# A unit's exponentials on ScalarE, taken ahead of the split of the next unit's loaded q and k

## The chip, the cores and the metric

One Trainium2 chip, one core of it. The metric is the device time of one execution in microseconds (us), lower is better; three runs of the kernel before are there, and one more execution under the profiler. TensorE, VectorE, ScalarE, GpSimd and SyncE stand as PE, DVE, ACT, POOL and SP.

## The reference, cut to what matters

Four layers, each a residual cross-attention followed by a residual feed-forward part, over x of 8 x 128 tokens x 512. Layers 0, 1 and 3 attend with 32 query heads on 8 key heads of width 128 (layer 0 with rotary positions, 1 and 3 with RMS-normed q and k):

```python
q = rope_or_rmsnorm(x @ Wq); k = rope_or_rmsnorm(ctx @ Wk); v = ctx @ Wv   # 32 / 8 / 8 heads of 128
probs = softmax(q @ k.T / sqrt(128) + mask)        # per batch and head, 128 x 128
x = x + tanh(gate) * (probs @ v) @ Wo
x = x + tanh(gate) * ffn(layernorm(x))
```

## The kernel before

An attention layer of this kind is done in 64 **units** u: one key head g (four query heads, so q is 128 x 512 and k is 128 x 128) for one batch b. Matmuls take each operand as a high and a low part (`_h`, `_l`: ScalarE copies the high part, and VectorE or GpSimd subtracts it from the source). What feeds a unit's score matmuls are `qT_h`, `qT_l` and both halves of `kT`.

The order on every engine is written out by hand, in numbers. Iteration i of the outer list holds steps of several units; `self.at(i, order, name, layer, u)` places a step, the steps of an iteration are sorted by `order`, and each of the five engine programs walks the same sorted list and issues what it has under that name. An engine therefore runs its own parts strictly in this order, and a wait at the head holds all that is behind it. A unit begins in its iteration i and ends some six iterations later.

For the 52 units u = 8 to 59 of layers 0, 1 and 3 (`TURNED_BY_DMA`) q, k and the probabilities are turned (transposed) by way of DRAM:

- i + 1: VectorE transposes 32 x 32 blocks of q and k into `xn` (`blocks_q`), SP stores them to `between_q` (`store_q`), and later loads them as `q_in` (`load_q`, order 72).
- i + 2: `split_k` at 13 and `split_q` at 13.5: ScalarE waits for the load, in layers 1 and 3 scales the keys in place (`q_in<-q_in`), copies `kT` and `qT_h`; VectorE makes the low part of `kT`, GpSimd `qT_l`. `scores` at 70.5 is on TensorE.
- i + 3: `mask` at 4 on VectorE (it writes S and the negated row maximum `nmx`); `exp` on ScalarE, four instructions, W and `den` from S and `nmx`; then `rden` on VectorE (it stands behind `times_v` there), the product `W<-W,rden` on GpSimd (`probs`, 40), its block transposition `S<-W` on VectorE (`blocks_p`, 42) and the store to `between_p` on SP (`store_p`, 42); `load_p` at 73.
- i + 4: `split_p` at 45 (`pT_h` on ScalarE, `pT_l` on GpSimd); i + 5: `times_v` at 20 (`oT_h` on ScalarE, `oT_l` on VectorE); i + 6: `attn_out` at 0 on TensorE.

So in one iteration ScalarE meets `exp` of unit u, the split of q and k of unit u + 1, and `oT_h` of unit u - 2; in the same iteration SP issues the store of unit u's probabilities, and behind it the load of q and k of unit u + 2. Weights come as halves of pieces into `raw` and are split to `ring_h` (ScalarE) and `ring_l` (GpSimd) by `next` steps, at 15 and 90 of an iteration in the steady part of a layer:

```python
for order in ((71, 90) if i < 7 else (15, 90) if i in self.steady else (5, 24, 46, 90)):
    self.at(i, order, "next", i + order / 100, "dve" if order == 46 else "pool")
```

During layer 0, every second iteration from 16 on also has `clear_slots` at 47: SP issues a DMA that clears 1030 KB of DRAM, ahead of `load_q`.

Of the kernel before, what the change touches and what calls it, by code (L numbers as in the profile page):

```python
# [91 lines left out]
class Schedule:  # L92
# [44 lines left out]
    def attention(self, layer, first, base):  # L137
        lag = 6
        units = [(g, b) for g in range(G) for b in range(NB)]
        self.first[layer], self.units[layer] = first, units  # L140
        for u, (g, b) in enumerate(units):
            i = first + u
            if b == 0:
                row = base + 5 * g
                keys_values, *queries = self.need((row + 2, row, row + 1), i, 70)
                five = [*queries, keys_values, *self.need(range(row + 3, row + 5), i + lag, 0)]
            self.five[layer, u] = five
            last = b == NB - 1
            ahead = (layer, u) in AHEAD
            early = layer == 3 and u < 2  # L150
            self.at(*((first - 1, 5) if early else (i, 45 if ahead else 70)), "keys_values", layer, u,
                    needs=[five[2], self.ctx[b]])
            self.at(i, 45 if ahead else 70, "project", layer, u, needs=five[0:2],
                    frees=[(n, "qkv", (layer, u), i + 0.7) for n in five[0:3]] if last else ())
            if KINDS[layer] == "norm":
                self.at(i + 1, 6 if layer == 1 and u < NB else 10, "normalise", layer, u)
            if (layer, u) in TURNED_BY_DMA:
                self.at(i + 1, 10.2 if KINDS[layer] == "norm" else 11, "blocks_q", layer, u)
                self.at(i + 1, 12, "store_q", layer, u)
                self.at(i + 1, 72, "load_q", layer, u)  # L160
                self.at(i + 2, 13, "split_k", layer, u)
                self.at(i + 2, 13.5, "split_q", layer, u)
                self.at(i + 2, 70.5, "scores", layer, u)
                self.at(i + 3, 4, "mask", layer, u)
                self.at(i + 3, 16, "exp", layer, u)
                self.at(i + 3, 40, "probs", layer, u)
                self.at(i + 3, 42, "blocks_p", layer, u)
                self.at(i + 3, 42, "store_p", layer, u)
                self.at(i + 3, 73, "load_p", layer, u)
                self.at(i + 4, 45, "split_p", layer, u)  # L170
            else:
                self.at(i + 1, 72 if (layer, u - 1) in TURNED_BY_DMA else 50, "turn_q", layer, u)
                self.at(i + 1, 72 if (layer, u - 1) in TURNED_BY_DMA else 50, "split_k", layer, u)
                self.at(i + 2, 40, "scores", layer, u)
                self.at(i + 2, 56, "mask", layer, u)
                self.at(i + 2, 71, "exp", layer, u)
                self.at(i + 3, 9, "probs", layer, u)
                if (layer, u) in TURNED_BY_PE:
                    self.at(i + lag - 2, 46 if u == 0 and (layer, 1) in AHEAD else 30, "turn_p", layer, u)
                else:  # L180
                    self.at(i + 3, 21, "blocks_p", layer, u)
                    self.at(i + 3, 21, "store_p", layer, u)
                    self.at(i + 3, 62, "load_p", layer, u)
                    self.at(i + lag - 2, 60, "split_p", layer, u)
            self.at(i + lag - 1, 20, "times_v", layer, u)
            self.at(i + lag, 0, "attn_out", layer, u, needs=five[3:5],
                    frees=[(n, "attn_out", (layer, u), i + lag) for n in five[3:5]] if last else ())
            self.at(i + lag, 10.5 if KINDS[layer] == "norm" or i + lag - 1 - first in range(NB, LAST_BY_DMA + 1) else 0,
                    "add_out", layer, u)
            if NB <= u < len(units) - NB:  # L190
                self.steady.add(i)
        return [first + units.index((G - 1, b)) + lag for b in range(NB)]
# [2467 lines left out]
```

## Time and profile before

| what | value |
|---|---|
| median of 3 runs | 2883.64 us (2881.02 to 2886.97) |
| the profiled execution | 2890.32 us, its span 2888.5 us |
| busy in the span: PE, DVE, POOL, ACT | 2438.5, 1860.4, 1553.4, 1213.2 us |
| TensorE's granted clock, mean | 0.935 |
| DMA | 390.33 MB, 135 GB/s |

The span is the time from the first to the last instruction in the trace. An engine's busy time says nothing of which wait sets the pace; idle times before an instruction and what released it do, and these are read per unit in the next parts.

### The profile page before, as it was taken

How to read it: one execution, taken by the hardware profiler on the slowest of the kernel's cores; microseconds unless marked ns; L12 is line 12 of the kernel's file. 1: busy time of each engine (PE TensorE's matmuls, PEld its weight loads, DVE VectorE, ACT ScalarE, POOL GpSimd, SP SyncE). 2: the span in 40 equal slices, each digit the busy share in tenths (PEclk: the TensorE clock that was granted, in tenths of full speed). 3: DMA queues.
4: the chain of work that ended last, by engine and by line, in shares of the span. 5: the costliest groups of instructions: out<-in, count | busy, mean ns of one | idle time of the engine just before them, and what ended most of it. 6: DMA issues, size and time to landing. Idle time of an engine off the chain costs nothing. (4 is left out here: it accounts for less than half of the span.)

```text
span 2888.5 us, 40547 instructions
## 1 busy us (share of the span) xinstructions
PE 2438.5 (84%) x12225; PEld 1996.1 (69%) x12225; DVE 1860.4 (64%) x3505; ACT 1213.2 (42%) x3610; POOL 1553.4 (54%) x1624
## 2 busy tenths in 40 slices
PE   5888888888888888889788888799788888889877
PEld 4777777676677777777666677676567777777753
DVE  4766666666887666666676676563376666666762
ACT  2433333333424455555542445323235555555420
POOL 4565565565424566666542666541446666666433
PEclk8998888889999999999999999899889999999989
DMA  3345555555313444444431000148624444444254
GB/s 103 94 157 176 169 194 172 177 172 172 126 63 116 156 147 146 148 150 149 139 128 45 16 1 1 42 161 310 241 63 138 149 152 152 148 142 144 93 194 164
DMA packets 296365, 390.33 MB, mean 135 GB/s; under 512 B 20977, under 2 KB 195697, under 8 KB 293210
## 3 DMA queue, kind: packets, MB, share of 16 engines
q1 hardware_dynamic: 280416, 338.60, 36.1%
q0 software_dynamic: 10224, 42.03, 4.2%
q10 hardware_dynamic: 5514, 7.11, 0.8%
q8 instruction: 105, 1.72, 0.2%
q14 instruction: 106, 0.87, 0.1%
HBM read 269.92 MB, written 151.49 MB: 146 GB/s over the span
## 5 line engine op out<-in xcount | busy, mean ns | idle before, releaser
L2252 POOL TENSOR_TENSOR qT_l<-q_in,qT_h 128x512 fp32r<-128x512 f32 x156 | 203.6, 1305 | 380.1 <-ACT qT_h L1197 379.3
L898 PE MATMUL B_s<-kT,qT_h 128*128 128x256 f32 x768 | 215.9, 358 | 174.5 <-POOL qT_l L2252 151.4
L1376 ACT ACTIVATE W<-S,nmx 128x128 f32<-128x128 f32 x768 | 297.6, 393 | 63.6 <-DVE nmx L1703 63.3
L1522 DVE TENSOR_TENSOR oT_l<-B_three,oT_h 128x512 fp32r<-128x512 f32 x200 | 137.2, 686 | 285.5 <-ACT oT_h L1197 285.3
L898 PEld LDWEIGHTS B_s<-kT,qT_h 128*128 128x128 f32 x768 | 154.8, 202 | 229.1 <-POOL qT_l L2252 198.7
L2292 POOL TENSOR_TENSOR W<-W,rden 128x512 f32<-128x512 f32 x192 | 200.1, 1042 | 204.9 <-DVE rden L1708 204.8
L841 PE MATMUL B_out<-ring_h,oT_h 128*128 128x512 f32 x516 | 230.6, 447 | 40.7 <-DVE oT_l L1522 34.8
L1197 ACT ACTIVATE q_in<-q_in,wqk 128x128 f32<-128x128 f32 x104 | 55.2, 531 | 488.2 <-DMA q_in<-between_q 488.2
L1718 DVE STREAM_TRANSPOSE S<-W 128x512 f32<-128x512 f32 x184 | 130.6, 710 | 188.0 <-POOL W L2292 187.8
L2298 POOL TENSOR_TENSOR pT_l<-W,pT_h 128x512 fp32r<-128x512 f32 x184 | 238.6, 1297 | 21.3 <-ACT pT_h L1197 21.2
L2228 POOL TENSOR_TENSOR ring_l<-raw,ring_h 128x512 fp32r<-128x512 f32 x166 | 214.3, 1293 | 62.7 <-ACT ring_h L1197 62.6
L841 PE MATMUL B_out<-ring_l,oT_h 128*128 128x512 f32 x516 | 217.6, 422 | 0.0
L841 PE MATMUL B_out<-ring_h,oT_l 128*128 128x512 f32 x516 | 216.7, 420 | 0.0
L1197 ACT ACTIVATE kT<-q_in 128x128 fp32r<-128x128 f32 x156 | 67.5, 433 | 353.0 <-DMA q_in<-between_q 349.7
L899 PE MATMUL B_s<-kT,qT_l 128*128 128x128 f32 x768 | 178.2, 232 | 0.0
L899 PEld LDWEIGHTS B_s<-kT,qT_l 128*128 128x128 f32 x768 | 158.4, 206 | 2.1
L841 PEld LDWEIGHTS B_out<-ring_h,oT_h 128*128 128x128 f32 x516 | 106.3, 206 | 74.0 <-DVE oT_l L1522 46.8
L2239 POOL TENSOR_TENSOR rn<-rn,pw 128x5 f32<-128x5 f32 x128 | 149.8, 1170 | 10.7
L1728 DVE SCALAR_TENSOR_TENSOR X<-B_out,gates,X 128x512 f32<-128x512 f32 x200 | 145.2, 726 | 11.4 <-PE B_out L841 11.4
L841 PE MATMUL B_qkv<-ring_h,xnT_h 128*128 128x512 f32 x348 | 142.8, 410 | 11.4 <-DVE spare_l L1522 4.8
L1376 ACT ACTIVATION_READ_ACCUMULATOR W<-S,nmx 128x1 f32 x768 | 144.8, 188 | 0.0
L1522 DVE TENSOR_TENSOR kT<-q_in,kT 128x128 fp32r<-128x128 f32 x156 | 84.2, 539 | 91.9 <-ACT kT L1197 91.9
(504 smaller groups left out, 7901.3 us busy)
## 6 DMA issues: line engine op xcount, KB each, us to landing
raw<-in_pieces SPq DMA_DIRECT2D x270, 256.0 KB
between_q<-xn SPq DMA_DIRECT2D x156, 320.0 KB, 2.9
q_in<-between_q SPq DMA_DIRECT2D x156, 320.0 KB, 3.2
between_p<-S SPq DMA_DIRECT2D x184, 256.0 KB, 2.1
W<-between_p SPq DMA_DIRECT2D x184, 256.0 KB, 3.0
slots_x<-in_zero SPq DMA_DIRECT2D x32, 1030.0 KB, 5.9
raw<-in_experts SPq DMA_DIRECT2D x16, 768.0 KB, 7.3
w<-in_experts SPq DMA_DIRECT2D x8, 1024.0 KB, 15.9
```

Of the source, the lines that this page charges most:

```text
L841: t = pe.matmul(dst, a, b, start=first and n == 0, stop=last and n == len(steps) - 1)
L898: pe.matmul(B_s[:, cols(r, 2 * P)], qT[0][:, cols(r)], kT_both[:, :], start=True, stop=False)
L899: t = pe.matmul(B_s[:, cols(2 * r)], qT[1][:, cols(r)], kT[0], start=False, stop=True)
L1376: t = act.activation(probs_r, scores_r, ACT.Exp, bias=nmx[:, k, r:r + 1], accum_out=den[:, k, r:r + 1])
L1522: return dve.tensor_tensor(dst, a, b, ALU.subtract)
L1718: dve.transpose(blocks_first(S[:, k, :]), W[:, k, :].rearrange("p (r j q) -> p r j q", r=R, q=BLOCK)).then_inc(*blocks_made.now((layer, u)))
L1728: dve.scalar_tensor_tensor(out=X[:, b, 0:D], in0=bank[:, :], scalar=factor, in1=X[:, b, 0:D], op0=ALU.mult, op1=ALU.add).then_inc(*x_add.n ...
L2228: pool.tensor_tensor(lo, landing_place(item), f32(hi), ALU.subtract).then_inc(*piece_lo["pool"].now(i))
L2239: pool.tensor_tensor(rn[:, k, 0:R + 1], rn[:, k, 0:R + 1], pw[:, 0:R + 1], ALU.pow).then_inc(*rms.now((layer, u)))
L2252: pool.tensor_tensor(heads_first(qT[1][:, :]), queries_in, heads_first(f32(qT[0][:, :])), ALU.subtract).then_inc(*q_low.now((layer, u)))
L2292: pool.tensor_tensor(W3, W3, rden[:, k, :].unsqueeze(2).to_broadcast([P, R, P]), ALU.mult).then_inc(*probs.now((layer, u)))
L2298: pool.tensor_tensor(heads_first(pT[1][:, :]), by_block(W[:, k, :]), heads_first(f32(pT[0][:, :])), ALU.subtract).then_inc(*p_split.now((l ...
```

## The change

One number of the list: `exp` of a unit that is turned by DMA goes from order 16 to 12.5 of the same iteration.

```diff
                 self.at(i + 2, 13.5, "split_q", layer, u)
                 self.at(i + 2, 70.5, "scores", layer, u)
                 self.at(i + 3, 4, "mask", layer, u)
-                self.at(i + 3, 16, "exp", layer, u)
+                self.at(i + 3, 12.5, "exp", layer, u)
                 self.at(i + 3, 40, "probs", layer, u)
```

No instruction is added or taken away. Only ScalarE has a part under `exp`; VectorE's `rden` goes by the step of its own. On ScalarE the four exponentials now stand ahead of the next unit's k and q (orders 13, 13.5) and of the weight split at 15. This holds for 153 units, 51 of each of the layers 0, 1 and 3; the orders of the other four engines are the same as before.

ScalarE in layer 0 before, two iterations, the first with a weight split at 15 and the second without (`B_three` is a PSUM bank, `ring_lent_h` the high part of weights):

```order
L1197 ACTIVATE kT<-q_in 128x128
L1197 ACTIVATE qT_h<-q_in 128x512
L1197 ACTIVATE ring_lent_h<-raw 128x512
L1376 ACTIVATE W,den<-S,nmx 128x128 x4
L1197 ACTIVATE oT_h<-B_three 128x512
L1197 ACTIVATE pT_h<-W 128x512
L1197 ACTIVATE v_h<-B_three 128x128
L1197 ACTIVATE kT<-q_in 128x128
L1197 ACTIVATE qT_h<-q_in 128x512
L1376 ACTIVATE W,den<-S,nmx 128x128 x4
```

The same engine and place in the changed kernel:

```order
L1376 ACTIVATE W,den<-S,nmx 128x128 x4
L1197 ACTIVATE kT<-q_in 128x128
L1197 ACTIVATE qT_h<-q_in 128x512
L1197 ACTIVATE ring_lent_h<-raw 128x512
L1197 ACTIVATE oT_h<-B_three 128x512
L1197 ACTIVATE pT_h<-W 128x512
L1197 ACTIVATE v_h<-B_three 128x128
L1376 ACTIVATE W,den<-S,nmx 128x128 x4
L1197 ACTIVATE kT<-q_in 128x128
L1197 ACTIVATE qT_h<-q_in 128x512
```

The four exponentials have passed the two copies of the next unit and the weight split; `oT_h` is behind all of them both times.

GpSimd in layer 1 (`rn` are the scales of the RMS norm), the same before and after; two iterations with a weight split between `qT_l` and W, then one without:

```order
L2252 TENSOR_TENSOR qT_l<-q_in,qT_h 128x512
L2228 TENSOR_TENSOR ring_lent_l<-raw,ring_lent_h 128x512
L2292 TENSOR_TENSOR W<-W,rden 128x512
L2298 TENSOR_TENSOR pT_l<-W,pT_h 128x512
L2236 TENSOR_SCALAR rn<-ss 128x5
L2239 TENSOR_TENSOR rn<-rn,pw 128x5
L2228 TENSOR_TENSOR ring_lent_l<-raw,ring_lent_h 128x512
L2252 TENSOR_TENSOR qT_l<-q_in,qT_h 128x512
L2292 TENSOR_TENSOR W<-W,rden 128x512
```

Nothing moves here: the product of unit u stands behind `qT_l` of unit u + 1, whose input ScalarE now makes later.

## Rows read from the trace of the kernel before

**Rows 1.** The page: the chain that ended last, by line

```profile
DMA q_in<-between_q 6%; POOL qT_l L2252 2%; POOL W L2292 2%; DMA out_x<-rows_last 2%; DMA slots_y<-S 1%; DVE S L1718 1%; PE B_qkv L841 1%; ACT qT_h L1197 1%; POOL ring_l L2228 1%; ACT q_in L1197 1%; DVE X L1728 1%; SPq L2437 1%; PE B_out L841 1%; POOL ring_lent_l L2228 1%; PE B_three L1093 1%
```

**Rows 2.** Waits in layer 1, 960 to 1300 us: total us, times, longest

```profile
POOL W L2292 <- DVE rden L1708: 35.2, 33, 1.6
PE B_s L898 <- POOL qT_l L2252: 28.5, 31, 5.3
```

**Rows 3.** Timeline, layer 1, iteration with weight split: start, us, instruction, [idle <-releaser]

```profile
1236.33 0.69 DVE L1703 TENSOR_REDUCE nmx<-S 128x4 f32<-128x512 f32 x1
...
1243.70 0.71 DVE L1718 STREAM_TRANSPOSE S<-W 128x512 f32<-128x512 f32 x1 [1.15 <-POOL W L2292]
...
1246.67 0.69 DVE L1703 TENSOR_REDUCE nmx<-S 128x4 f32<-128x512 f32 x1
...
1237.68 0.53 ACT L1197 ACTIVATE q_in<-q_in,wqk 128x128 f32<-128x128 f32 x1 [4.50 <-DMA q_in<-between_q]
...
1239.62 0.39 ACT L1376 ACTIVATE W<-S,nmx 128x128 f32<-128x128 f32 x1
...
1241.16 0.58 ACT L1197 ACTIVATE oT_h<-B_three 128x512 fp32r<-128x512 f32 x1
...
1248.16 0.53 ACT L1197 ACTIVATE q_in<-q_in,wqk 128x128 f32<-128x128 f32 x1 [4.63 <-DMA q_in<-between_q]
...
1242.62 1.04 POOL L2292 TENSOR_TENSOR W<-W,rden 128x512 f32<-128x512 f32 x1 [0.74 <-DVE rden L1708]
```

**Rows 4.** Timeline, layer 1, the iteration ahead of it, without weight split

```profile
1226.45 0.69 DVE L1703 TENSOR_REDUCE nmx<-S 128x4 f32<-128x512 f32 x1
...
1227.85 0.53 ACT L1197 ACTIVATE q_in<-q_in,wqk 128x128 f32<-128x128 f32 x1 [5.07 <-DMA q_in<-between_q]
...
1230.81 0.58 ACT L1197 ACTIVATE oT_h<-B_three 128x512 fp32r<-128x512 f32 x1
...
1232.28 1.04 POOL L2292 TENSOR_TENSOR W<-W,rden 128x512 f32<-128x512 f32 x1 [1.53 <-DVE rden L1708]
```

**Rows 5.** Timeline of PE in the same two iterations

```profile
1230.81 0.39 PE L898 MATMUL B_s<-kT,qT_h 128*128 128x256 f32 x1 [0.62 <-POOL qT_l L2252]
...
1232.17 0.50 PE L841 MATMUL B_out<-ring_h,oT_h 128*128 128x512 f32 x1 [0.23 <-DVE oT_l L1522]
...
1240.70 0.39 PE L898 MATMUL B_s<-kT,qT_h 128*128 128x256 f32 x1 [0.63 <-POOL qT_l L2252]
...
1242.52 0.50 PE L841 MATMUL B_out<-ring_h,oT_h 128*128 128x512 f32 x1 [0.68 <-DVE oT_l L1522]
```

**Rows 6.** Timeline, layer 0, no clear ahead of the load: without and with weight split

```profile
608.46 0.69 DVE L1703 TENSOR_REDUCE nmx<-S 128x4 f32<-128x512 f32 x1
...
608.90 0.43 ACT L1197 ACTIVATE kT<-q_in 128x128 fp32r<-128x128 f32 x1 [5.11 <-DMA q_in<-between_q]
...
612.77 1.04 POOL L2292 TENSOR_TENSOR W<-W,rden 128x512 f32<-128x512 f32 x1 [1.53 <-DVE rden L1708]
...
658.16 1.04 POOL L2292 TENSOR_TENSOR W<-W,rden 128x512 f32<-128x512 f32 x1 [0.75 <-DVE rden L1708]
```

**Rows 7.** Timeline, layer 0, a clear ahead of the load: with and without weight split

```profile
603.49 1.04 POOL L2292 TENSOR_TENSOR W<-W,rden 128x512 f32<-128x512 f32 x1 [0.84 <-DVE rden L1708]
...
617.75 0.69 DVE L1703 TENSOR_REDUCE nmx<-S 128x4 f32<-128x512 f32 x1
...
621.75 0.43 ACT L1197 ACTIVATE kT<-q_in 128x128 fp32r<-128x128 f32 x1 [7.51 <-DMA q_in<-between_q]
...
624.14 0.57 ACT L1197 ACTIVATE oT_h<-B_three 128x512 fp32r<-128x512 f32 x1
...
625.60 1.04 POOL L2292 TENSOR_TENSOR W<-W,rden 128x512 f32<-128x512 f32 x1 [1.56 <-DVE rden L1708]
```

**Rows 8.** PE's timeline, then windows (us, busy of PE, PEld, DVE, ACT, POOL, PEclk, DMA)

```profile
1335.97 0.65 PE L841 MATMUL B_out<-ring_h,oT_h 128*128 128x512 f32 x1 [0.78 <-DVE oT_l L1522]
...
1336.20:1339.50 3.30, 3.30 (x9) 2.52 (x9) 2.31 (x5) 0.26 (x2) 2.92 (x4) 0.50 0.48 160
```

## The prediction

> **What bounds the kernel now.** I began with the chain that ended last: its largest line is the load of q and k from DRAM, 6% of the span [rows 1], so the units turned by DMA are the place to look. The waits of a stretch of layer 1 show that GpSimd waits for `rden` in every one of 33 iterations, 35.2 us in all, and that TensorE waits for `qT_l` in 31 of them, 28.5 us [rows 2]. Then I followed one iteration in the timeline. q lands at 1237.68; the scaling, `kT`, `qT_h` and a weight split run until the first exponential at 1239.62; `oT_h` starts at 1241.16, 1.54 us later; `rden` and the product W follow at 1242.62, the block transposition at 1243.70 to 1244.41, and 3.75 us after its end the next q is there, at 1248.16 [rows 3]. That is a closed cycle of 10.48 us: load, split, exponentials, product, transposition, store, load. The four exponentials lie in it with 1.54 us.
>
> They need not. They wait for `nmx`, and VectorE ends it at 1247.36, 2.95 us after the same transposition [rows 3]. Call d the time from the end of `nmx` to the arrival of q. It is 0.80 us here and 0.66 in the iteration ahead of it (1237.68 less 1237.02) [rows 3]. Both ends hang on the transposition, so d will not change much when the cycle does.
>
> **The change step by step.** No work is added; one block of 1.54 us changes places with the split, on ScalarE alone. Two things follow in an iteration.
>
> *The `rden` side.* Before, exponentials end at q + K + 1.54, where K is the time of the split (1.42 us in rows 4 after taking 1.54 from 1230.81 less 1227.85; 1.94 with a weight split, 1239.62 less 1237.68 in rows 3). After, `oT_h` starts at the later of (nmx + 0.04 + 1.54) and q, plus K; the 0.04 is my allowance for the semaphore. So `oT_h`, `oT_l`, `rden` come d earlier, at most 1.54; with d below 0 they come later.
>
> *The `qT_l` side.* `qT_h` waits for the exponentials, so it and `qT_l` on GpSimd come later by δ = 1.58 - d, or 0 if q is later than that. W stands behind `qT_l`, and behind `ring_l` where the iteration has a weight split, and GpSimd was idle for a time g ahead of W. W can therefore come forward by the smaller of (gain of `rden`) and (g - δ). The rest of the cycle starts with W, so this is the gain of the iteration.
>
> Layers 1 and 3, no weight split: q at 1227.85, `nmx` ends 1227.14, d = 0.71, δ = 0.87, g = 1.53 [rows 4]: the smaller of 0.71 and 0.66. Over the 34 such iterations with d between 0.38 and 1.06 this averages 0.72: **24.6 us**.
> With weight split: d = 0.66, δ = 0.92, g = 0.74 [rows 3]: W comes 0.18 us *later*. Where d is 0.80 it is about level. Over 55 iterations the average is -0.10: **-5.2 us**. Here the weight split on GpSimd eats what ScalarE gives.
> Seven iterations of these layers have q over 2 us late (the first ones of a layer among them): 4 without split give 1.55, 3 with it 0.84: **8.7 us**. Six near the ends have `nmx` later than q, and lose 0.2 to 1.5: **-4.6 us**.
>
> Layer 0 has two kinds in turn. With a clear ahead of the load, q lands at 621.75 while `nmx` ended at 618.44 [rows 7]: the exponentials are over long before, δ is 0, and `oT_h` goes from 624.14 to 622.60. Without weight split GpSimd's idle 1.56 us lets W follow by 1.54 to 1.56, with one the idle 0.84 us is all that there is [rows 7]. 7 x 1.55 + 17 x 0.79 = **24.3 us**.
> Without a clear, VectorE has rotary products to do ahead of the mask and q is *earlier* than `nmx`: 608.90 against 609.15, d = -0.25 [rows 6]. Then δ = 1.83, and W moves by 1.53 - 1.83 = -0.30; with a weight split (idle 0.75) by -1.1 [rows 6]. 15 iterations average -0.38 and 12 average -1.07: **-18.5 us**.
>
> Sum: 24.6 - 5.2 + 8.7 - 4.6 + 24.3 - 18.5 = 29.3 us less. The counts and averages are over all 153 iterations, with each one's own d and g; the rows are typical ones.
>
> *What could eat it on TensorE.* Its work in an iteration is 1240.70 less 1230.81 less the idle 0.63 and 0.23, so 9.03 us [rows 5]. The iteration without split goes from 9.83 (1237.68 less 1227.85) to some 9.17: it still fits, barely. Scores start δ later, but they had idle time behind them at `attn_out`, 0.68 us with the split and 0.23 without [rows 5], and the mask that needs them is far: `nmx` starts at 1246.67 behind two mask steps of 0.7 us each, so the mask at about 1245.2, while the scores started at 1240.70 [rows 3, 5] and take 1.2. So I price it at nothing, and if that cover fails it is the second rival.
> What remains is the clock. The idle times of 0.63 and 0.68 around the scores become one of about 1.4 us ahead of them. Before, TensorE was at 1.2 GHz (granted 0.50) for 1336.20 to 1339.50, behind an idle time of 0.78 us and one like it just before [rows 8]; so idle time of this sum does drop it now and then, and then half of 3.3 us of work is lost, 1.65, of which the iteration with split has 10.4 - 9.0 = 1.4 spare. At one in ten of the 55, 0.3 us each, that is 2 us. I take 1.5.
>
> From the profiled execution's 2890.32 us (span 2888.5 and 1.8 around it) this gives 2862.5; the median of the runs is 6.7 us below it, so I forecast 2883.64 - 28 = **2856 us**.
>
> **Rivals.**
> *GpSimd's order doesn't hold it (W follows `rden` alone).* Then every iteration of layers 1 and 3 gains d, with split too: 89 x 0.72 = 64, and the late ones 31 x 1.54 = 48, less 27 x 0.30 + 5 = 13: some 100 us, 2784. For it: W is released by `rden` in all 33 iterations [rows 2]. Against: it comes after `qT_l` in the list, and with idle of 0.74 against a delay of 0.92 `rden` is no longer the last. The Trainium skill says in "Perfetto Trace Analysis", Tensor Engine Instruction, that ScalarE, VectorE and GpSimd are strict FIFO, which would exclude this; no row of before shows W ready and held. 0.03.
>
> *TensorE sets the pace (slower).* The place is the start of the scores. If each δ there is passed on, less the idle at `attn_out`, the iterations with split lose 0.88 - 0.68 = 0.20, 55 x 0.20 = 11 us, and those without 0.83 - 0.23 = 0.60, 34 x 0.60 = 20: 31 us slower, 2915. It decides where the projection's end, not `qT_l`, releases the next scores; now `qT_l` does, after 0.62 us idle [rows 5], and TensorE has 1.4 us to spare in an iteration with split. What speaks for it is 31 waits of 33 for `qT_l` [rows 2]: they are where TensorE loses time, and the change makes them longer. The Trainium skill's advice in the same page, Optimization Strategies, is of this kind: speed up what keeps the matmul engine waiting. By that advice this change is the wrong way round. The cycle in rows 3 says otherwise, since `scores` isn't in it. 0.12.
>
> *Gains and losses cancel.* If d shrinks by 0.3 us everywhere (loads landing earlier against VectorE, or `nmx` late by scores), 89 iterations of layers 1 and 3 lose 0.3 each from both sides, 27 us, and nothing is left: 2883. The averages with split and in layer 0 show how near zero many are. 0.10.
>
> *Clock.* If half of the 55 iterations with split fall to 1.2 GHz, and each loses 0.3, and the neighbours without split, which have nothing spare, take the full 1.65 in one of four: 8 + 14 us, 2878. 0.10.
>
> **How the numbers follow.** My forecast has 0.65 and its own range is 2846 to 2868 (d off by 0.1 moves it by 9; layer 0's losses by half, 9). The range of 2840 to 2890 takes in cancelling and the clock and leaves out most of the slower rival and the 100 us one. A difference under 0.2%, 6 us, can't be told from none. Faster: 0.65 + 0.03 + 0.09 of the clock case and a little of cancelling, 0.78. Same 0.09, slower 0.13.
>
> **What would show it.** In the changed trace: ScalarE's exponentials released by `nmx` and ended before q or at most 1 us behind it; W released by `qT_l` or `ring_l` with no idle time in iterations with split, and nearly so without; periods of 9.2 us without split in layer 1 and an unchanged 10.4 with; in layer 0 the iteration behind a clear shorter by 0.8 to 1.5, the other longer by 0.3 to 1.1; TensorE idle 1.3 us ahead of the scores and nearly none ahead of `attn_out`. I would be wrong if d turns out to shrink, if the scores come to be released by the projection in most iterations, or if the 0.50 clock spreads in layers 1 and 3.

## The result and the profile after

The changed kernel takes 2849.43 us (median of 4 runs, 2841.56 to 2853.46); the kernel before, on the same chip, 2882.33 us. The ratio is 0.9883, with an interval of 0.9855 to 0.991: 1.2% less, 33 us. The profiled execution took 2853.46 us, 36.9 less than that of before.

The page of the changed kernel: span, busy times, the chain that ended last (by engine, by line), and two of its groups of instructions.

```profile
span 2851.6 us, 40547 instructions
...
PE 2408.4 (84%) x12225; PEld 1979.2 (69%) x12225; DVE 1849.1 (65%) x3505; ACT 1220.0 (43%) x3610; POOL 1543.3 (54%) x1624
...
ACT W L1376 5%; POOL qT_l L2252 4%; PE B_qkv L841 4%; POOL W L2292 4%; DMA slots_y<-S 3%; DVE S L1700 2%; DVE ss L1614 2%; DVE nmx L1703 2%; ACT qT_h L1197 2%; DVE S L1697 2%; DMA q_in<-between_q 2%; DMA out_x<-rows_last 2%; ACT q_in L1197 2%; PE B_out L841 1%; POOL ring_l L2228 1%
...
L1376 ACT ACTIVATE W<-S,nmx 128x128 f32<-128x128 f32 x768 | 300.3, 397 | 775.9 <-DVE nmx L1703 775.8
...
L2292 POOL TENSOR_TENSOR W<-W,rden 128x512 f32<-128x512 f32 x192 | 199.9, 1041 | 39.2 <-DVE rden L1708 38.5
```

The load of q led the chain with 6% [rows 1]; it has 2% now, and the exponentials (`W L1376`), `qT_l` and the product W stand at the top. The exponentials' idle time is released by `nmx`, nearly all of it. The product's idle time is 39.2 us over its 192 units, where the page of before has 204.9.

The waits of layer 1, 960 to 1300 us, changed kernel (total us, times, longest):

```profile
ACT W L1376 <- DVE nmx L1703: 145.7, 34, 5.0
POOL qT_l L2252 <- ACT qT_h L1197: 107.6, 34, 4.0
DVE S L1718 <- POOL W L2292: 52.5, 34, 1.8
...
PE B_s L898 <- POOL qT_l L2252: 32.3, 29, 2.4
```

The wait of the product for `rden`, 35.2 us in 33 iterations [rows 2], is gone: it has no row any more. TensorE's wait for `qT_l` is longer in sum, 32.3 us where [rows 2] have 28.5.

Two iterations of layer 1 in the timeline of the changed kernel, with a weight split, then without one:

```profile
1179.74 0.40 ACT L1376 ACTIVATE W<-S,nmx 128x128 f32<-128x128 f32 x1 [4.52 <-DVE nmx L1703]
...
1181.30 0.53 ACT L1197 ACTIVATE q_in<-q_in,wqk 128x128 f32<-128x128 f32 x1
...
1182.89 1.26 POOL L2252 TENSOR_TENSOR qT_l<-q_in,qT_h 128x512 fp32r<-128x512 f32 x1 [2.62 <-ACT qT_h L1197]
1183.24 0.57 ACT L1197 ACTIVATE oT_h<-B_three 128x512 fp32r<-128x512 f32 x1
...
1184.12 1.28 POOL L2228 TENSOR_TENSOR ring_l<-raw,ring_h 128x512 fp32r<-128x512 f32 x1
1184.21 0.39 PE L898 MATMUL B_s<-kT,qT_h 128*128 128x256 f32 x1 [1.58 <-POOL qT_l L2252]
...
1185.37 1.03 POOL L2292 TENSOR_TENSOR W<-W,rden 128x512 f32<-128x512 f32 x1
...
1186.43 0.71 DVE L1718 STREAM_TRANSPOSE S<-W 128x512 f32<-128x512 f32 x1 [1.81 <-POOL W L2292]
...
1189.40 0.69 DVE L1703 TENSOR_REDUCE nmx<-S 128x4 f32<-128x512 f32 x1
...
1190.12 0.40 ACT L1376 ACTIVATE W<-S,nmx 128x128 f32<-128x128 f32 x1 [4.51 <-DVE nmx L1703]
...
1191.68 0.52 ACT L1197 ACTIVATE q_in<-q_in,wqk 128x128 f32<-128x128 f32 x1
...
1193.26 1.30 POOL L2252 TENSOR_TENSOR qT_l<-q_in,qT_h 128x512 fp32r<-128x512 f32 x1 [2.61 <-ACT qT_h L1197]
1194.55 1.04 POOL L2292 TENSOR_TENSOR W<-W,rden 128x512 f32<-128x512 f32 x1
```

ScalarE's first instruction on q (`q_in<-q_in`, which scales the keys) starts right behind the last exponential, with no idle time: the 4.50 us of waiting for the load [rows 3] have moved ahead of the exponentials, where they are a wait for `nmx`. On GpSimd `qT_l`, `ring_l` and W now run back to back (1182.89 to 1186.40), so the product has no slack left. The iteration without a split has lost its 1.53 us of idle time [rows 4] too. TensorE waits 1.58 us ahead of the scores where [rows 5] have 0.63.

The rows from one product to the next, 1185.37 to 1194.55, also show what sets the pace now. W and its transposition are over at 1187.14; VectorE ends the mask steps and `nmx` at 1190.09; the exponentials run to 1191.68; scaling, `kT` and `qT_h` until `qT_l` starts at 1193.26; W follows at 1194.55. That is a second closed cycle, of 9.18 us, with no load in it, and with a weight split `ring_l` is in it too, 1.25 us (1184.12 to 1185.37), which makes 10.4. The exponentials have left the cycle of the load, but they are in this one. In layers 1 and 3, 28 of the 34 iterations without a split lie within 0.05 us of 9.20, and 48 of the 55 with one within 0.05 us of 10.38; ScalarE still waited for the load in 7 of these 89, where before it did in all of them. The chain that ended last, from 2300 to 2400 us (layer 3), before and then after:

```profile
by line: DMA q_in<-between_q 31.6%; issue 16.7%; POOL qT_l L2252 13.3%; POOL W L2292 10.5%; DVE S L1718 7.2%; ACT qT_h L1197 6.3%; ACT q_in L1197 5.4%; POOL ring_l L2228 5.1%; SPq L2437 3.2%; POOL ring_lent_l L2228 1.2%; SPq L2457 0.3%; ACT
...
by line: issue 17.0%; POOL qT_l L2252 12.7%; ACT W L1376 12.4%; POOL W L2292 10.5%; DVE ss L1614 7.0%; DVE S L1700 6.3%; DVE nmx L1703 6.3%; ACT qT_h L1197 6.2%; DVE S L1697 5.5%; DMA q_in<-between_q 4.8%; ACT q_in L1197 4.0%; POOL ring_l L
```

Layer 0 in the changed kernel: an iteration without a clear ahead of its load, then one behind a clear.

```profile
601.74 0.40 ACT L1376 ACTIVATE W<-S,nmx 128x128 f32<-128x128 f32 x1 [6.03 <-DVE nmx L1703]
...
603.30 0.41 ACT L1197 ACTIVATE kT<-q_in 128x128 fp32r<-128x128 f32 x1
...
604.31 1.29 POOL L2252 TENSOR_TENSOR qT_l<-q_in,qT_h 128x512 fp32r<-128x512 f32 x1 [1.93 <-ACT qT_h L1197]
605.60 1.04 POOL L2292 TENSOR_TENSOR W<-W,rden 128x512 f32<-128x512 f32 x1
...
611.30 0.40 ACT L1376 ACTIVATE W<-S,nmx 128x128 f32<-128x128 f32 x1 [5.69 <-DVE nmx L1703]
...
614.54 0.43 ACT L1197 ACTIVATE kT<-q_in 128x128 fp32r<-128x128 f32 x1 [1.59 <-DMA q_in<-between_q]
...
616.86 1.04 POOL L2292 TENSOR_TENSOR W<-W,rden 128x512 f32<-128x512 f32 x1
```

Behind the clear the exponentials are over 1.59 us before q lands, where q came after 7.51 us of idle time and the exponentials followed it [rows 7]. In the other kind ScalarE is held by `nmx` until 601.74, and the copies stand behind the exponentials.

I measured each iteration as the time from the product W ahead of it to its own. Averages by kind, us, before and after:

| kind of iteration | count | before | after | sum | forecast |
|---|---|---|---|---|---|
| layers 1 and 3, no weight split | 34 | 9.92 | 9.32 | -20.3 | -24.6 |
| layers 1 and 3, weight split | 55 | 10.42 | 10.46 | +2.3 | +5.2 |
| layers 1 and 3, q over 2 us behind `nmx` | 7 | | | -11.4 | -8.7 |
| layers 1 and 3, near the ends | 6 | | | +2.3 | +4.6 |
| layer 0 behind a clear, no split | 7 | 13.50 | 11.88 | -11.4 | -24.3 with the next row |
| layer 0 behind a clear, split | 17 | 14.16 | 13.14 | -17.3 | |
| layer 0 without a clear, no split | 15 | 9.42 | 9.77 | +5.3 | +18.5 with the next row |
| layer 0 without a clear, split | 12 | 9.79 | 10.76 | +11.7 | |

The sum is 38.8 us less; over the same iterations, from product to product, the stretch of layer 0 went from 593.9 to 582.2 us, that of layer 1 from 550.6 to 535.8, that of layer 3 from 530.5 to 518.0, together 39.0. The other stages gave back 2.

### The profile page after: what moved, and what is told of

Read it like the earlier page. It is cut to its first block, busy times and chain, and to the rows that moved or that the text cites. A ratio compares the mean times of both kernels' runs of the same rounds, so it can differ in the third digit from the quotient of the medians.

```text
span 2851.6 us, 40547 instructions
## 1 busy us (share of the span) xinstructions
PE 2408.4 (84%) x12225; PEld 1979.2 (69%) x12225; DVE 1849.1 (65%) x3505; ACT 1220.0 (43%) x3610; POOL 1543.3 (54%) x1624
## 4 chain that ended last, share of the span: by engine, by line
DVE 15%; POOL 14%; PE 11%; issue 10%; ACT 10%; DMA 8%; ACTq 0%; SPq 0%; DVEq 0%; POOLq 0%
ACT W L1376 5%; POOL qT_l L2252 4%; PE B_qkv L841 4%; POOL W L2292 4%; DMA slots_y<-S 3%; DVE S L1700 2%; DVE ss L1614 2%; DVE nmx L1703 2%; ACT qT_h L1197 2%; DVE S L1697 2%; DMA q_in<-between_q 2%; DMA out_x<-rows_last 2%; ACT q_in L1197 2%; PE B_out L841 1%; POOL ring_l L2228 1%
## 5 line engine op out<-in xcount | busy, mean ns | idle before, releaser
L1376 ACT ACTIVATE W<-S,nmx 128x128 f32<-128x128 f32 x768 | 300.3, 397 | 775.9 <-DVE nmx L1703 775.8
L898 PE MATMUL B_s<-kT,qT_h 128*128 128x256 f32 x768 | 217.2, 360 | 220.2 <-POOL qT_l L2252 196.6
L2298 POOL TENSOR_TENSOR pT_l<-W,pT_h 128x512 fp32r<-128x512 f32 x184 | 238.5, 1296 | 20.3 <-ACT pT_h L1197 20.2
L2292 POOL TENSOR_TENSOR W<-W,rden 128x512 f32<-128x512 f32 x192 | 199.9, 1041 | 39.2 <-DVE rden L1708 38.5
L1522 DVE TENSOR_TENSOR kT<-q_in,kT 128x128 fp32r<-128x128 f32 x156 | 61.3, 393 | 143.1 <-ACT kT L1197 143.1
L841 PE MATMUL B_qkv<-ring_h,xnT_h 128*128 128x512 f32 x348 | 142.5, 409 | 11.4 <-DVE spare_l L1522 4.8
L1376 ACT ACTIVATION_READ_ACCUMULATOR W<-S,nmx 128x1 f32 x768 | 144.5, 188 | 0.0
L1197 ACT ACTIVATE ring_h<-raw 128x512 fp32r<-128x512 f32 x190 | 117.5, 624 | 61.9 <-DMA raw<-in_pieces 37.8
L841 PE MATMUL B_qkv<-ring_l,xnT_h 128*128 128x512 f32 x348 | 140.4, 404 | 0.0
L841 PE MATMUL B_qkv<-ring_h,xnT_l 128*128 128x512 f32 x348 | 138.9, 399 | 0.0
```

The costliest lines, as they stand in the source:

```text
L841: t = pe.matmul(dst, a, b, start=first and n == 0, stop=last and n == len(steps) - 1)
L898: pe.matmul(B_s[:, cols(r, 2 * P)], qT[0][:, cols(r)], kT_both[:, :], start=True, stop=False)
L1197: return act.activation(dst, src, ACT.Copy, scale=scale)
L1376: t = act.activation(probs_r, scores_r, ACT.Exp, bias=nmx[:, k, r:r + 1], accum_out=den[:, k, r:r + 1])
L1522: return dve.tensor_tensor(dst, a, b, ALU.subtract)
L2292: pool.tensor_tensor(W3, W3, rden[:, k, :].unsqueeze(2).to_broadcast([P, R, P]), ALU.mult).then_inc(*probs.now((layer, u)))
```

## The experiments

The change edits line 165. "Before" is the kernel before, run on the same chip as each.

**One layer kind at a time.** `e1_norm_only` makes the change in layers 1 and 3 alone:

```diff
-                self.at(i + 3, 12.5, "exp", layer, u)
+                self.at(i + 3, 16 if layer == 0 else 12.5, "exp", layer, u)
```

> The exponentials go ahead of the split in layers 1 and 3 alone; layer 0 as before. Theory (each iteration gains the smaller of d and g less delta): the trace after gives 27 us of gain in layers 1 and 3 (my sum before had 23.5), so about 2855 us against 2882 before. Rival (layer 0's late loads give most of it): 2870 or more.

Measured: 2858.12 us, ratio 0.9908 (0.9875 to 0.9942), 29 us less. Layers 1 and 3 were as in the full change (9.32 and 9.24 us without a split, 10.38 and 10.40 with one), layer 0 as before. `e2_rope_only` makes it in layer 0 alone:

```diff
-                self.at(i + 3, 12.5, "exp", layer, u)
+                self.at(i + 3, 12.5 if layer == 0 else 16, "exp", layer, u)
```

> The exponentials go ahead in layer 0 alone. Theory: iterations behind a clear gain 0.8 to 1.6 us (24 of them, 24 to 29 us), the others lose 0.3 to 1.1 (17 us): net 6 to 12 us, about 2873. Rival (layer 0's losses are hidden by TensorE, so only gains count): 2857.

Measured: 2881.32 us, ratio 0.9981 (0.9961 to 1.0002), some 6 us less, an interval that just includes no change. By kind layer 0 gained and lost as in the full change (-11.6 and -14.8 behind a clear, +5.3 and +11.7 without). So layer 0 nearly cancels, and layers 1 and 3 give most of the result; 29 and 6 add up to 35, beside the 33 of the whole.

**Only where it helps.** `e6_behind_clear` keeps the new order in layers 1 and 3 and behind a clear, and the old one in the rest of layer 0:

```diff
-                self.at(i + 3, 12.5, "exp", layer, u)
+                self.at(i + 3, 16 if layer == 0 and i % 2 else 12.5, "exp", layer, u)
```

> The changed kernel, but in layer 0 the exponentials stay at 16 in the iterations whose load of q has no clear ahead of it (units with odd i). Theory: there q comes before nmx is done, so the new order only delays qT_h and loses 0.35 and 1.0 us in 15 and 12 iterations, 17 us; leaving it out gives 2849 - 17, about 2832 us. Rival (the loss and the gain of neighbours hang together): 2849.

Measured: 2834.96 us, ratio 0.9811 (0.9785 to 0.9837). The iterations without a clear were back at 9.37 and 9.85 us, those behind one stayed at 11.69 and 13.23. The loss of 17.0 us in the table above comes from the order there: taking it back gave 14 us by the medians, 21 by the ratios.

**Is it the weight split that eats the gain?** The split of a weight stands at order 15, between `qT_l` and the product on GpSimd. I moved it behind the product, in the kernel before (`e3_split_behind_w`) and in the changed one (`e4_both`):

```diff
-            for order in ((71, 90) if i < 7 else (15, 90) if i in self.steady else (5, 24, 46, 90)):
+            for order in ((71, 90) if i < 7 else (41, 90) if i in self.steady else (5, 24, 46, 90)):
```

> The kernel before, with the weight split of the steady iterations at order 41 instead of 15, so that ring_h stands behind oT_h on ScalarE and ring_l behind the product W on GpSimd. Theory of the closed cycle: ScalarE's 0.52 us of ring_h leaves the cycle in the 87 iterations with a split, and GpSimd's 1.3 us was in none (it was idle 0.74 us ahead of W): 45 us faster, about 2837. Rival (TensorE sets the pace): no change, 2882.

> The changed kernel with the weight split at order 41 as well. Theory (in the changed kernel an iteration with split is held by qT_l and ring_l on GpSimd, no longer by rden): iterations with split come to the period of those without, 10.46 to 9.32 us in 55 of layers 1 and 3, and about 1 us each in 29 of layer 0: some 90 us below the changed kernel's 2849, 2760. Rival (GpSimd's order is no limit, W follows rden alone): only ring_h's 0.52 us, 2805. Rival (TensorE sets the pace already): 2849.

Measured: `e3_split_behind_w` 2998.31 us, ratio 1.0388 (1.0356 to 1.042), slower where I expected faster; `e4_both` 2819.07 us, 0.9777 (0.974 to 0.9814), half of the gain over before that I expected. The trace of `e3_split_behind_w` shows what I had not counted: a step's DMA moves with it. Its timeline (SPq is the queue on which SyncE issues):

```profile
1240.23 1.28 POOL L2228 TENSOR_TENSOR ring_l<-raw,ring_h 128x512 fp32r<-128x512 f32 x1
...
1241.54 0.33 SPq L2430 DMA_DIRECT2D raw<-in_pieces  x1
...
1241.97 0.38 SPq L2437 DMA_DIRECT2D between_p<-S  x1
...
1242.46 0.37 SPq L2463 DMA_DIRECT2D q_in<-between_q  x1
...
1246.44 0.53 ACT L1197 ACTIVATE q_in<-q_in,wqk 128x128 f32<-128x128 f32 x1 [5.79 <-DMA q_in<-between_q]
```

The weight split issues the load of the next raw weight piece, which may overwrite `raw` only when `ring_l` is done at 1241.51. At order 41 it stands ahead of the store at 42, and the store of S, ready at 1241.02, is issued at 1241.97. q is used 5.4 us after the transposition's end instead of 3.75 [rows 3]. The edit had put a wait into the cycle of the load.

So `e8_before_43` and `e7_after_43` repeat it with 43 in place of 41, behind the store:

> The kernel before, weight split of the steady iterations at 43: behind the product W on GpSimd and behind the store of the probabilities on SP. My theory of order 41 failed by 160 us; what I now hold is that the raw load, which waits for ring_l, stood ahead of the store on SP and put store and next load 1.7 us back. With 43 the store is free and only the load of q waits some 0.4 us behind the raw load, about what ring_h gives back on ScalarE: 2875 to 2885. Rival (it is GpSimd's later pT_l, or ring_h ahead of pT_h, that costs): still over 2950.

> The changed kernel with the weight split at 43. Theory (GpSimd's order holds W back by ring_l in iterations with split, and order 41 gave back half of that on SP): their period falls to that without split, 10.45 to 9.3 us in 55 of layers 1 and 3, somewhat less in 29 of layer 0: 2770 to 2785. Rival (SP's raw load isn't what held order 41): 2819 as there.

Measured: `e8_before_43` 2915.13 us, 1.0086 (1.0055 to 1.0117); `e7_after_43` 2771.14 us, 0.9596 (0.9571 to 0.9621). `e7_after_43` is as expected; `e8_before_43` is 30 us above the 2885 that I gave as its upper end. With the split of the weight out of its way, the iteration with one went to 9.48 and 9.54 us in layers 1 and 3 of `e7_after_43`, beside 10.46 in the changed kernel. ScalarE's part of the weight split moved too, but that is 0.52 us, less than the 0.95 gained; and in the changed kernel `rden` was done 0.76 us ahead of W on average in these 55 iterations, while `ring_l` ran. That shows the step "the weight split on GpSimd eats what ScalarE gives". The same move of the exponentials is worth 1.2% with the weight split at 15 and 4.9% (0.9596 against 1.0086; 144 us by the medians) with it at 43.

Why `e8_before_43` still lost some 25 us, in its timeline:

```profile
1254.71 0.33 SPq L2437 DMA_DIRECT2D between_p<-S  x1
...
1255.22 0.33 SPq L2430 DMA_DIRECT2D raw<-in_pieces  x1
...
1255.66 0.41 SPq L2463 DMA_DIRECT2D q_in<-between_q  x1
...
1259.35 0.53 ACT L1197 ACTIVATE q_in<-q_in,wqk 128x128 f32<-128x128 f32 x1 [5.03 <-DMA q_in<-between_q]
```

The raw load now stands between the store and the load of q: 0.95 us from one issue to the other where it was 0.43, and 3.69 us from the issue to the use where it was 3.29. Over layers 1 and 3 it is alike: from the issue of the load of q to its landing the median is 3.71 us in the 56 loads with a raw load just ahead, and 3.22 in 101 loads of the kernel before. That is some 1.0 us more in the cycle of the load, against the 0.52 us that ScalarE's part of the split gives back: an estimate of 0.5 us each in 55 iterations, some 27 us in all, beside the 27.5 that this trace lost in the 89 ordinary iterations of these layers. In `e7_after_43` most of the same delay is hidden behind the exponentials; ScalarE waited for q in 32 of the 89, under 0.2 us on average over all.

**The rest of the chain ahead too.** If the exponentials needn't follow q, the sums, `rden`, the product, the transposition and the store needn't either. `e9_rden_w_ahead` moves the step that makes `rden` and W ahead of the split, the first of the three lines; `e5_w_ahead` the transposition and the store as well:

```diff
-                self.at(i + 3, 40, "probs", layer, u)
-                self.at(i + 3, 42, "blocks_p", layer, u)
-                self.at(i + 3, 42, "store_p", layer, u)
+                self.at(i + 3, 12.6, "probs", layer, u)
+                self.at(i + 3, 14, "blocks_p", layer, u)
+                self.at(i + 3, 14, "store_p", layer, u)
```

> The changed kernel with rden and the product W ahead of the next unit's split too (probs at 12.6, block transposition and store of the probabilities at 14). Theory (the exponentials are ready early, and only the order behind them keeps W back): W starts 0.3 us after the last exponential, the cycle through the load falls under TensorE's 9.03 us of work, and TensorE sets the pace at 9.1 to 9.3 us in all of layers 1 and 3: 75 us there, and 40 to 70 in layer 0, 2700 to 2735. Rival (TensorE or contention is near its limit already): above 2800.

> The changed kernel with rden and W at 12.6 only; block transposition and store stay at 42. Theory: W's place behind qT_l and ring_l was the hold; the transposition then waits for oT_l instead, 2.1 to 2.6 us after the last exponential where W is done at 1.35, and the store stands behind the raw load on SP. TensorE is the bound in layers 1 and 3 as before that costs anything: 2670 to 2710. Rival (order 14 of the transposition and the store is what gave the gain): above 2780.

Measured: `e5_w_ahead` 2666.88 us, 0.9237 (0.9207 to 0.9267), more than expected; `e9_rden_w_ahead` 2717.59 us, 0.9421 (0.9386 to 0.9456), a little above what was expected. From the timeline of `e5_w_ahead`:

```profile
1106.11 0.39 PE L898 MATMUL B_s<-kT,qT_h 128*128 128x256 f32 x1
...
1110.12 0.40 ACT L1376 ACTIVATE W<-S,nmx 128x128 f32<-128x128 f32 x1 [2.96 <-DVE nmx L1703]
...
1112.49 1.04 POOL L2292 TENSOR_TENSOR W<-W,rden 128x512 f32<-128x512 f32 x1 [3.12 <-DVE rden L1708]
...
1112.69 1.00 DVE L1522 TENSOR_TENSOR kT<-q_in,kT 128x128 fp32r<-128x128 f32 x1 [0.28 <-ACT kT L1197]
...
1113.49 1.35 POOL L2252 TENSOR_TENSOR qT_l<-q_in,qT_h 128x512 fp32r<-128x512 f32 x1
...
1114.89 0.39 PE L898 MATMUL B_s<-kT,qT_h 128*128 128x256 f32 x1
```

The product starts 2.37 us after the start of the first exponential; in the changed kernel it started 5.63 after it (1185.37 less 1179.74), for it stood behind `qT_l` and `ring_l`. The scores follow one another after 8.78 us, and TensorE has no idle time ahead of them. By kind, layers 1 and 3 take 9.26 and 8.85 us without a split, 8.78 and 8.89 with one. What left the cycle through `nmx` are `qT_l` and `ring_l`, which W no longer stands behind. This is where TensorE becomes the bound: it is busy 89% of the span, and in layer 1 the chain that ended last is its work alone, here from 1000 to 1100 us:

```profile
by line: PE B_out L841 32.3%; PE B_three L841 25.0%; PE B_qkv L841 22.0%; PE B_s L898 10.3%; PE B_three L918 7.7%; PE B_s L899 2.9%; issue 0.0%
```

`e10_w_ahead_exp16` puts the exponentials back behind the split and leaves the rest of `e5_w_ahead`; what follows them in the program now holds `qT_l`:

```diff
-                self.at(i + 3, 12.5, "exp", layer, u)
+                self.at(i + 3, 16, "exp", layer, u)
```

> W, transposition and store ahead as in the 2667 us kernel, but the exponentials at 16 as in the kernel before. Theory: the exponentials are then in the load's cycle again, and qT_l, behind W, is 2.5 us later than before, so that TensorE waits for it: between 2850 and 2950, most of the gain gone. Rival (the place of W alone made the gain, the exponentials' place does little): below 2720.

Measured: 2948.85 us, 1.0213 (1.018 to 1.0246), just inside the range expected, but slower than before where I expected most of the gain gone. Its waits, 980 to 1500 us:

```profile
ACT q_in L1197 <- DMA q_in<-between_q: 198.9, 47, 9.7
POOL W L2292 <- DVE rden L1708: 191.5, 47, 9.3
...
PE B_s L898 <- POOL qT_l L2252: 66.4, 34, 8.0
```

GpSimd stands at the product, waiting for exponentials that wait for a load, in all 47 iterations, and `qT_l` and the scores wait behind it. The two orders belong together: to move `rden`, W, the transposition and the store costs 2.1% with the old order of the exponentials and gives 6.5% more with the new one (0.9237 against 0.9883).

**The clear out of the way.** What remained in layer 0 was the clear, which stands ahead of the load of q on its queue. `e11_clear_last` is `e5_w_ahead` with it later:

```diff
-                self.at(16 + 2 * n, 47, "clear_slots", n)
+                self.at(16 + 2 * n, 74, "clear_slots", n)
```

> The 2667 us kernel with the clear of 1030 KB behind the loads of q and W on SP (order 74 instead of 47). Theory: layer 0's q comes late because the clear is ahead of its load; without it layer 0 comes nearer to TensorE's 9 us, 508 us of units to some 480: 2640. Rival (the clear takes the same DMA time wherever it stands, and then delays the store of q and of the probabilities): 2667.

Measured: 2612.87 us, ratio 0.906 (0.9029 to 0.9092), the best version of this study, 9.4% less than before. Its page (busy times, then the chain by engine) and a window of its layer 0 (us, busy of PE, PEld, DVE, ACT, POOL, then TensorE's granted clock, DMA share, GB/s):

```profile
span 2608.6 us, 40547 instructions
...
PE 2343.7 (90%) x12225; PEld 1933.7 (74%) x12225; DVE 1940.0 (74%) x3505; ACT 1231.1 (47%) x3610; POOL 1548.7 (59%) x1624
...
PE 33%; POOL 9%; DVE 9%; DMA 8%; issue 7%; ACT 3%; SPq 0%; ACTq 0%; POOLq 0%; DVEq 0%
...
150.00:590.00 440.00, 427.73 (x2312) 361.04 (x2310) 382.20 (x643) 220.65 (x703) 335.04 (x306) 1.00 0.69 226
```

The same view of the changed kernel, layer 0 and layer 1:

```profile
85.00:738.00 653.00, 550.12 (x2750) 458.91 (x2750) 414.88 (x761) 255.58 (x823) 385.54 (x358) 0.93 0.52 169
...
905.00:1500.00 595.00, 518.56 (x2690) 432.30 (x2689) 411.87 (x706) 311.27 (x918) 359.77 (x351) 0.96 0.47 149
```

The 51 iterations of layer 0 take 460.3 us where the changed kernel takes 582.2; TensorE is busy for 427.73 of 440 us at its full 2.4 GHz, where it stood at 0.93 of it on average. In the same 440 us `e5_w_ahead` has a granted clock of 0.96. How much of the gain beyond the 2640 expected is the clock, and how much the shorter waits, was not tried apart.

## Why the prediction was right, point by point

The time, 2849.43 us, lies in the forecast's own range (2846 to 2868), and the mechanism is the one forecast; the table and the experiments bear it out.

*The cycle.* Load, split, exponentials, product, transposition, store, load: the exponentials left it. Shown by the timeline after (exponentials ahead of q, no idle time between them and the first instruction on it); and in the kernel before, where this cycle sets the pace, 1.0 us more on the way from the store to q (`e8_before_43`) made it 25 us slower. What the forecast doesn't say in words is that a second cycle then sets the pace, and that the exponentials are in it: W, transposition, `nmx`, exponentials, split, `qT_l`, `ring_l`, W, 9.2 us or 10.4. Its sum has it all the same: q + 1.58 - d is the end of the exponentials, the time from which δ and g - δ count, so g - δ is the old period less the new one. `e9_rden_w_ahead` took `qT_l` and `ring_l` out of this second cycle and was 132 us faster than the change.

*The smaller of two gains.* W follows `rden` or GpSimd's queue, whichever is later. The forecast held that d would stay; from the end of `nmx` to the landing of q it was 0.73 us before and 0.74 after on average without a split, 0.69 and 0.84 with one. In iterations without a split both were near 0.7, and 0.60 was measured (20.3 in place of 24.6); with one it should lose 0.10, and lost 0.04 (2.3 in place of 5.2). The idle time ahead of W, which the forecast called g, is used up in both kinds, as forecast. The periods were forecast as 9.2 and 10.4 and are 9.3 and 10.5.

*Late q and layer 0.* The seven late ones gave 11.4 in place of 8.7, the 24 behind a clear 28.7 in place of 24.3: with a split I had capped the gain at GpSimd's idle 0.84 us and 1.02 was measured. The same 17 iterations gave 0.87 in `e2_rope_only` and 0.94 in `e6_behind_clear`, so part of the other 0.2 is how the loads fell in one execution; the rest is not settled. Without a clear the loss was 17.0 in place of 18.5, so the negative d (q at 608.90 against `nmx` at 609.15) led to the right loss.

*TensorE.* Priced at nothing, and it cost nothing that shows: over the whole kernel its waits for `qT_l` ahead of the scores went from 151.4 to 196.6 us, the idle time ahead of the first matmul of `attn_out` from 40.7 to 7.2, and the periods follow the product. The clock, priced at a loss of 1.5 us, can't be told from nothing: over the units the granted clock was 0.96 before and after in layer 1, 0.98 and 0.97 in layer 3, and it rose from 0.89 to 0.93 in layer 0. It does fall behind such a wait at times. A window of the changed kernel, behind the scores at 1184.21 (us, busy of PE, PEld, DVE, ACT, POOL, clock, DMA share, GB/s):

```profile
1185.97:1189.75 3.78, 3.78 (x11) 3.00 (x10) 3.25 (x6) 0.00 (x0) 3.39 (x5) 0.56 0.66 189
```

That is mostly the 1.2 GHz level, behind the 1.58 us of idle time. The iteration from W at 1185.37 to W at 1194.55 still took 9.18 us, like its neighbours, though it has no weight split: the forecast's rival had such ones pay the full 1.65 us.

*The rivals.* "GpSimd's order doesn't hold it" is refuted: W has no wait for `rden` any more and stands flush behind `ring_l`; moving `ring_l` from ahead of it (`e7_after_43`), or `qT_l` and `ring_l` (`e5_w_ahead`), is worth 78 and 183 us by the medians. The trace of before had a sign of it too, though the forecast saw no such row: in three iterations, the last with a weight split of each layer, W starts without idle time behind `ring_l` or `ring_lent_l`, 1.03 us after `rden` was done. The rule of the Trainium skill, "Perfetto Trace Analysis", Tensor Engine Instruction, that these engines take their instructions in strict order, agrees with these traces: in the 55 iterations with a split `rden` was done 0.76 us ahead of W on average, and W passed `ring_l` in none. "TensorE sets the pace" is refuted for this change: it would have been 31 us slower. Layers 1 and 3 come to it with `e5_w_ahead`. "Gains and losses cancel" holds in layer 0 alone (`e2_rope_only`, 0.9981), not in the whole. "Clock" did not come: it would have been 2878 us.

*What was left out.* The forecast treated the DMA issues as fixed, since the change moved none. My first experiment on the split then moved one without counting it, and missed by 161 us (2837 expected, 2998.31 measured).

## What to carry to other kernels

Where each engine takes its instructions in order, find the closed cycle in the timeline and ask of each step in it whether it needs the load that it follows. Moving it ahead gives only as much as the next engine's queue has idle time ahead of the step that uses its result, less what the move delays in that queue: in other words, until the next closed cycle sets the pace. Look for that one before the edit, and move the whole chain on every engine at once: alone the two halves gave -1.2% and +2.1% here, together -7.6%. And of a step that is moved, look at its DMA issues first: one load that waits for a buffer cost 3.0% ahead of one store, against the place behind it (1.0388 against 1.0086).

## What the runs showed of the hardware

VectorE's `kT` low part, 128 x 128, takes 0.38 us in the changed kernel at 1182.33, before GpSimd begins its `qT_l`, and 1.00 us in `e5_w_ahead` at 1112.69, where GpSimd's product runs from 1112.49 to 1113.53. In `e5_w_ahead` the median is 0.39 us for the 20 that no long GpSimd instruction touches, and 1.02 us for the 117 that fall wholly within such ones. What of the two engines' work collides was not tried by itself. The first row is this:

```profile
1182.33 0.38 DVE L1522 TENSOR_TENSOR kT<-q_in,kT 128x128 fp32r<-128x128 f32 x1 [0.38 <-ACT kT L1197]
```

The load of q took some 0.5 us longer from issue to landing when a raw weight load was issued 0.44 us ahead of it: a median of 3.71 us over 56 loads of layers 1 and 3 in `e8_before_43`, against 3.22 over 101 in the kernel before and 3.19 over the other 40 of `e8_before_43`.
